# Attention stage: the turns of the outputs and of the row of maxima move from the maxima's banks to the scores' banks, and from VectorE to ScalarE and GpSimd

## The reference, cut to what matters

```python
q = (x @ wq.T).reshape(B, S, num_heads, D)      # B 2, S 2048, 16 heads, D 16; k and v alike
scores = jnp.einsum('bqhd,bkhd->bhqk', q, k) * scale
probs = jax.nn.softmax(scores, axis=-1)
out = jnp.einsum('bhqk,bkhd->bqhd', probs, v).reshape(B, S, H)
return out @ wo.T
```

## Time and profile before

| | us |
|---|---|
| median of three timed runs | 3472.24 |
| the profiled execution, its own time | 3464.76 |
| its span | 3464.1 |
| attention stage, first exponential to last write of `att` | 1270.9 to 2765.3 |

### The profile page before, as it was taken

The page is one execution under the profiler, slowest core; times in us unless marked ns, Lnnn a source line. Parts: engine busy times, 40 slices in busy tenths (PEclk is TensorE's granted clock), DMA queues, the critical chain, the costliest instruction groups (busy, mean ns, idle before and its releaser), DMA issues. The chain is left out here.

```text
span 3464.1 us, 45140 instructions
## 1 busy us (share of the span) xinstructions
PE 2931.5 (85%) x12880; PEld 1119.1 (32%) x12881; DVE 2463.2 (71%) x2802; ACT 1877.2 (54%) x3418; POOL 1049.5 (30%) x556
## 2 busy tenths in 40 slices
PE   5799899888776869999999999999999872999990
PEld 1234344433333412222222222222222252566650
DVE  0699999999995588888887888888888364111113
ACT  3656665666542427776776767676677710222220
POOL 2888878877861610000000000000000035100006
PEclk8999999999988969999999999999999975999995
DMA  1111111111112521111111111111111036111114
GB/s 41 43 49 55 38 49 55 49 40 49 49 37 74 184 64 38 34 30 31 29 38 38 38 38 29 38 37 38 29 27 29 14 113 230 48 45 45 45 36 144
DMA packets 123092, 185.24 MB, mean 53 GB/s; under 512 B 30224, under 2 KB 77968, under 8 KB 122896
## 3 DMA queue, kind: packets, MB, share of 16 engines
q1 hardware_dynamic: 109072, 142.95, 14.6%
q0 software_dynamic: 13824, 39.86, 3.6%
HBM read 138.01 MB, written 44.43 MB: 53 GB/s over the span
## 5 line engine op out<-in xcount | busy, mean ns | idle before, releaser
L1446 DVE TENSOR_REDUCE nmh<-ring 128x2 f32<-128x1024 f32 x1024 | 1191.0, 1218 | 242.3 <-PE ring L1336 241.1
L1323 ACT ACTIVATE prob<-s_ps 128x512 f32<-128x512 f32 x2048 | 1066.9, 601 | 479.2 <-PE s_ps L1360 478.2
L767 DVE TENSOR_TENSOR_SCAN h<-dA,state,bx 128x512 f32<-128x512 f32 x512 | 618.6, 1268 | 115.3 <-ACT dA L606 114.7
L391 POOL TENSOR_TENSOR bx<-u,bb 128x2048 f32<-128x2048 f32 x128 | 578.8, 4528 | 194.2 <-DVE h L767 194.0
L1360 PE MATMUL s_ps<-qs,ks 98*128 98x512 bf16 x2048 | 600.9, 390 | 21.4 <-issue 13.7
L1372 PE MATMUL acc<-prob,vst 128*32 128x512 f32 x4096 | 557.0, 616 | 0.7 <-ACT prob L1323 0.7
L606 ACT ACTIVATE dA<-dt,aneg 128x512 f32<-128x512 f32 x512 | 348.8, 691 | 271.1 <-DVE h L767 271.0
L673 PE MATMUL y_ps<-h,ident 128*128 128x512 f32 x1024 | 491.2, 625 | 1.1 <-DVE h L774 1.1
L1336 PE MATMUL ring<-k,q 64*128 64x512 bf16 x2048 | 375.5, 398 | 106.7 <-DVE att L1470 40.2
L1311 POOL COPY vst<-v_all 128x544 f32 (+1 forms) x16 | 10.2, 641 | 1358.4 <-PE acc L1372 1358.4
L1360 PEld LDWEIGHTS s_ps<-qs,ks 98*128 98x128 bf16 x2048 | 152.7, 98 | 508.7 <-ACT prob L1323 398.8
(11 more groups left out here) (218 smaller groups left out, 2466.0 us busy)
## 6 DMA issues: line engine op xcount, KB each, us to landing
bb<-b_rows SPq DMA_DIRECT2D x128, 256.0 KB, 3.1
q<-parts SPq DMA_DIRECT2D x256, 64.0 KB, 2.1
parts<-part POOLq DMA_DIRECT2D x48, 256.0 KB, 3.1
qs<-parts SPq DMA_DIRECT2D x192, 64.0 KB, 2.9
ks<-parts SPq DMA_DIRECT2D x192, 64.0 KB, 3.0
xt<-slots_in POOLq DMA_DIRECT2D x72, 128.0 KB, 2.3
slots_out<-yt SPq DMA_DIRECT2D x72, 128.0 KB, 1.7
k<-parts SPq DMA_DIRECT2D x256, 32.0 KB, 1.9
```

Source lines behind the costliest of these rows:

```text
L391: nc.gpsimd.tensor_tensor(bx[:, n % BR], u[:, b], bb[:, n % RB, None, :].to_broadcast([P, KI, CH]), ALU.mult).then_inc(s_bx, 1)
L767: nc.vector.tensor_tensor_scan(h[:, n % HR, d, :], dA[:, d % 2, :], bx[:, n % BR, d, :], state[:, b, n, d:d + 1], ALU.mult, ALU.add).then_ ...
L1323: nc.scalar.activation(prob[:, k % PR, j, :], s_ps[:, m % SR, :], ACT.Exp, scale=SC).then_inc(s_exp, 1)
L1446: nc.vector.tensor_reduce(nmh[:, slot, t, 2 * s:2 * s + 2], ring[:, s, :, :], AX.X, ALU.max, negate=True).then_inc(s_free[s], 1)
```

## The change

Both turns leave the ring and take their place in the sequence of score tiles. Each head now has `TILES` = 66 bank uses, 64 score tiles, tile `I_OUT` = 12 for the outputs' transposes and tile `I_ROW` = 53 for the transpose of the maxima, all on the three banks of `s_ps` in turn. ScalarE copies each turn out to SBUF (`oraw`, `rowf`) and counts it with the exponentials; it copies `acc` out, too. VectorE keeps the combination to `nm` and the reciprocal (from `oraw`). GpSimd makes the two bfloat16 parts of the row and the product into `att`; its copy of v's columns is made in the second head of the pair before. The diff, cut to its core (`taken` is the count of the exponential or copy that takes a tile; the special cases of the first and last head are left out):

```diff
+        T_OUT, T_ROW = 2, KT - LEAD
+        I_OUT = QC * (T_OUT + 1)
+        I_ROW = QC * (T_ROW + 1) + 1
+        TILES = QC * KT + 2
...
-            if has_prev:
-                steps[2].append((OUT, 0))
...
-                steps[KT - LEAD].append((ROWMAX, 0))
...
+        def tile_of(t, j):
+            return QC * t + j + (1 if t > T_OUT else 0) + (1 if t > T_ROW else 0)
...
+        def bank_free(head, tile):
+            back = tile - SR
...
+            return taken(head, back)
...  SyncE
-            def max_rows(par, hh, fills):
-                wait_apart(sp, s_free[0], fills, s_one)
+            def max_rows(head, par, hh):
+                wait_apart(sp, s_nmr, head + 1, s_one)
...  GpSimd
+            def rows_of_max(head, tiles, sent):
+                wait_apart(pool, s_exp, tiles, s_id)
+                if sent is not None:
+                    wait_apart(pool, sent[0], sent[1], s_id)
+                nc.gpsimd.tensor_copy(nmr[:, 0, :], rowf[:, :]).then_inc(s_hi, 1)
+                wait_apart(pool, s_hi, head + 1, s_id)
+                nc.gpsimd.tensor_tensor(nmr[:, 1, :], rowf[:, :], nmr[:, 0, :], ALU.subtract).then_inc(s_nmr, 1)
+
+            def outputs(n, hh):
+                wait_apart(pool, s_rec, 2 * n + hh + 1, s_id)
...
+                nc.gpsimd.tensor_tensor(dst, got[:, :, :, 0:HD], r[:, :, :, None].to_broadcast([P, TT, QC, HD]),
+                                        ALU.mult).then_inc(s_on, 1)
...
             def head(n, it, par, hh, has_prev, has_next, has_then):
-                if hh == 0:
-                    wait_apart(pool, s_pv, KK * (n - 1), s_id)
...
+                if hh == 1 and has_next:
+                    wait_apart(pool, s_pv, KK * n, s_id)
+                    columns(n + 1, 1 - par)
+                if has_prev:
+                    outputs(n if hh == 1 else n - 1, 1 - hh)
+                if has_next:
+                    rows_of_max(2 * n + hh + 1, taken(2 * n + hh, I_ROW), (s_mr[hh], 32 * (n + 1)))
...  ScalarE
+            def read_acc(n, hh):
+                wait(act, s_pv, KK * n + KT * (hh + 1))
+                nc.scalar.copy(osb[:, hh, :], acc[:, :]).then_inc(s_o, 1)
+
+            def take_output(head, tile, nth):
+                wait(act, s_S, taken(head, tile))
+                wait(act, s_on, nth)
+                nc.scalar.copy(oraw[:, :], s_ps[:, tile % SR, :]).then_inc(s_exp, 1)
+
+            def take_row(head, tile, nth):
+                wait(act, s_S, nth if tile < 0 else taken(head, tile))
+                wait(act, s_nmr, nth - 1)
+                nc.scalar.copy(rowf[:, :], s_ps[0:KT, tile % SR, 0:P]).then_inc(s_exp, 1)
...
+                    if t == 1 and has_prev:
+                        read_acc(n if hh == 1 else n - 1, 1 - hh)
...  the four exponentials of key tile t
+                    if t == T_OUT and has_prev:
+                        take_output(u, I_OUT, u - 1)
+                    if t == T_ROW and has_next:
+                        take_row(u, I_ROW, u + 2)
...  TensorE
+            def rows_of_max(head, tile, nth):
+                wait(pe, s_exp, bank_free(head, tile))
+                wait(pe, s_comb, nth)
+                nc.tensor.transpose(s_ps[0:KT, tile % SR, 0:P], nm[:, :], ident[:, :]).then_inc(s_S, 1)
+            def outputs(free, tile, n, hh):
+                wait(pe, s_exp, free)
                 wait(pe, s_o, 2 * n + hh + 1)
...  the four transposes, now into s_ps[:, tile % SR, ...], counted in s_S
                     scores(n, par, k, 2)
                     scores(n, par, k, 3)
+                    turn(t)
                     values_of_last(k)
...  VectorE
-                nc.vector.tensor_copy(nmr[:, 0, :], ring[0:KT, 0, 0, 0:P]).then_inc(s_nmr1, 1)
...  and the subtraction, the product into att and the copy of acc
+            def reciprocals(tiles, n, hh):
+                wait(dve, s_exp, tiles)
+                wait(dve, s_on, 2 * n + hh - 1)
...
+                    if t == T_OUT + 1 and has_prev:
+                        reciprocals(taken(u, I_OUT), n if hh == 1 else n - 1, 1 - hh)
```

More of the change, by code:

```diff
@@ L1181, in attention_stage, with plan @@
         LOADS4 = 16 * 2 * 2 * 4
-        MAXNEXT, MAXTHEN, ROWMAX, OUT = "maximum, next head", "maximum, head after", "rows of the maximum", "output"
-        def plan(has_prev, has_next, has_then):
+        MAXNEXT, MAXTHEN = "maximum, next head", "maximum, head after"
+        T_OUT, T_ROW = 2, KT - LEAD
+        I_OUT = QC * (T_OUT + 1)
+        I_ROW = QC * (T_ROW + 1) + 1
+        TILES = QC * KT + 2
+        assert TILES % SR == 0 and I_ROW - I_OUT > SR
+        def plan(has_next, has_then):
             steps = [[] for _ in range(KT)]
-            if has_prev:
-                steps[2].append((OUT, 0))
             if has_next:
@@ L1281, in head @@
                 if has_next:
[L1282 to L1291, removed]
+                    max_rows(2 * n + hh + 1, *next_head(n, par, hh)[1:])
             every_head(sp, prologue, head)
@@ L1315, in _ @@
+            every_head(pool, prologue, head)
+            outputs(NP - 1, 1)
         @block.scalar
         def _(act):
-            def head(n, it, par, hh, has_prev, has_next, has_then):
-                for k in range(hh * KT, (hh + 1) * KT):
+            def read_acc(n, hh):
[5 more added lines that the diff above has]
+                nc.scalar.copy(oraw[:, :], s_ps[:, tile % SR, :]).then_inc(s_exp, 1)
@@ L1368, in values @@
                     wait(pe, s_vst, n + 1)
-                wait(pe, s_exp, NU * n + QC * (k + 1))
+                wait(pe, s_exp, taken(2 * n + hh, tile_of(t, QC - 1)))
                 for j in range(QC):
@@ L1404, in use_ring, with turn @@
                             maxima(ct, hh, at, s)
[L1405 to L1409, removed]
+                def turn(t):
+                    if t == T_OUT and has_prev:
+                        outputs(bank_free(u, I_OUT), I_OUT, n if hh == 1 else n - 1, 1 - hh)
+                    if t == T_ROW and has_next:
+                        rows_of_max(u, I_ROW, u + 2)
                 def values_of_last(k):
@@ L1435, in epilogue @@
                 values(NP - 1, 1, KK - 1)
-                ct = Count(2 * NP - 1, last=True)
-                ct.next(1)
-                outputs(ct, NP - 1, 1)
+                outputs(TILES * 2 * NP - 1, 0, NP - 1, 1)
             every_head(pe, prologue, head, epilogue)
@@ L1447, in maxima, with rows_of_max @@
                                         negate=True).then_inc(s_free[s], 1)
-            def rows_of_max(ct, n, hh, sent):
+            def rows_of_max(ct, slot, turned):
                 for s in range(2):
                     wait(dve, s_free[s], ct.n[s])
[L1452 to L1455, removed]
-                nc.vector.tensor_copy(nmr[:, 0, :], ring[0:KT, 0, 0, 0:P]).then_inc(s_nmr1, 1)
[L1457 to L1464, removed]
+                wait(dve, s_exp, turned)
+                nc.vector.tensor_reduce(nm[:, :], nmh[:, slot, :, :], AX.X, ALU.min).then_inc(s_comb, 1)
+            def reciprocals(tiles, n, hh):
+                wait(dve, s_exp, tiles)
+                wait(dve, s_on, 2 * n + hh - 1)
+                got = oraw[:, :].rearrange("p (c j w) -> p c j w", c=TT, j=QC)
                 r = rec[:, hh, :].rearrange("p (c j) -> p c j", j=QC)
                 nc.vector.reciprocal(r, got[:, :, :, HD]).then_inc(s_rec, 1)
[L1467 to L1476, removed]
             def prologue():
```

106 lines of the change are left out of this document (58 added, 48 removed).

## The result

The changed kernel takes 3385.74 us (median of 4, 3382.51 to 3388.28), the kernel before 3472.59 on the same chip: the ratio is 0.9751, 95% interval 0.9737 to 0.9765. The profiled execution took 3382.51 us, its span is 3381.1, 83.0 less than before.

A forecast was written before the change was run, and what follows sets the result against it. TensorE's own row of work was taken to bound the undisturbed period; 40.2 + 28.8 + 9.6 + 14.2 = 92.8 us off 3464.76 gave 3372, with 7.5 us for the median 3379.5, say 3380 us; range 3360 to 3420.

The forecast's parts named there:

- Undisturbed period: Two key tiles of a head without a turn: 5.28 us, TensorE's own row of work, not touched by the change.
- Outputs' turn: Period with the outputs' transposes: 0.72 us extra in place of 2.06, gain 1.34 us in 30 heads, 40.2 us.
- Row's turn: Period with the transpose of the maxima: 0.30 us extra in place of 1.23, 0.93 us in 31 heads, 28.8 us.
- Copies on ScalarE: Copies of `acc`, outputs and row moved to ScalarE: 0.59 us each large, about 0.28 the row; ScalarE does not become the bound.
- The row's way: Row to `qs` through ScalarE, GpSimd and SyncE: lands at 7.0 us, 8.2 at the slowest, wanted at 11.1; no cost.
- The rival's place: Rival that the row comes late: TensorE waits for it at each head's start, kernel slower, up to 3507 us; chance 0.04.
- GpSimd: Product into `att` 0.57 us, the row's two operations 0.4 us each, all off the path; no cost.
- The wrap: Pair boundary, where a bank wraps too soon: 0.64 us saved 15 times, 9.6 us, since 66 tiles divide by 3.
- The clock: Nine drops of TensorE's clock behind outputs' stalls in the loop go: 9 x 1.58 = 14.2 us, the least certain term.
- its first rival: The clock keeps dropping: drops hang on the back edge and work around it, not the stall; 3394 us, chance 0.15.
- The ends: Start about 0.9 us less, end about 0.9 us more for a second ScalarE copy and hand-over: even.

The follow-up runs named there:

- the late row: The changed kernel with one added GpSimd operation of two inputs on 128 x 4096 elements ahead of the parts of the row: 3480.68 us, ratio 1.0026.
- the bank order: The kernel before with only the order of its three score banks changed, from score tile 10 of a pair on: 3468.98 us, ratio 0.9995.
- the new engines in the old place: The kernel before with ScalarE copying both turns and `acc` out and GpSimd finishing, both turns still in the ring: 3445.37 us, ratio 0.9928.
- the turns one place later: The changed kernel with each turn behind the values on TensorE instead of ahead of them: 3369.64 us, ratio 0.9703.

## Why the prediction was right

The forecast was 3380 us, the measurement 3385.74. Against the profiled execution the sum said 92.8 us; the span fell by 83.0. By the prediction's own steps:

- **Undisturbed period, 5.28 us, TensorE's own.** Right: eight periods of 5.28 us and what the two turns add make 42.24 + 0.75 + 0.37 = 43.36, the head measured.
- **Outputs' turn, 0.72 us for 2.06.** Measured 0.75. 30 x 1.31 = 39.3 us for 40.2. The transposes start 2.05 us into the period (2.06 reckoned), and the values follow them after 0.59 (0.55).
- **Row's turn, 0.30 us for 1.23.** Measured 0.37, 31 x 0.86 = 26.7 us for 28.8. The transposing instruction took 0.21 us to the next load (1391.63 to 1391.84), not the 0.13 taken over from the outputs.
- **Copies on ScalarE cost nothing.** Shown for the two large ones by doubling them: not even twice the work shows.
- **The row's way.** DMAs out at 3.93 us where 4.1 were reckoned, landing 1.7 us in the median again. The slack was reckoned at 4.1 us (11.1 - 7.0); the late row shows 4.6 in the mean. The rival's place was right: once the row is late enough, TensorE waits for it at the head's start.
- **GpSimd.** The product took 619 ns for the 570 taken, the parts of the row 279 and 417 for 400 each. The Trainium skill (GPSIMD Engine Reference, Elementwise — side-by-side cycle accounting) has GpSimd about two times slower with two inputs, measured there on 2048 elements. Here the product takes 619 ns for VectorE's 425 and the subtraction 417 for 278, a factor of 1.5; the cast, with one input, takes 279 ns on both. VectorE read PSUM and GpSimd reads SBUF, so this is not the same operation in all. It is off the path either way.
- **The wrap, 0.64 us.** 0.58 by the two traces of the bank order, 8.7 us for 9.6.
- **The clock, 14.2 us.** The weakest term, as said. All nine drops behind the outputs' stall went, as forecast, and with the stalls of 0.81 us they are gone, too. But the excess fell by 36.5 - 25.6 = 10.9 us only, as the heads with back edges have become no cheaper, rather some 2.5 us dearer in all. Two readings behind this term were wrong. The window 1590 to 1600 of the earlier trace rows is not of an unrolled head: the first back edge comes at 1638.87, so it lies in the loop's first pass. And only four of the five back edges are followed by a drop at once. What that window shows is a stall in the loop without a drop; the stalls of the unrolled heads, which the prediction held in favour of its first rival, are shorter (1.20 to 1.26 us). Nor do the drops belong to particular heads. There were 9 in the kernel before, 14 with another bank order, 3 with the loop written out, 1 with both.
- **The ends.** Taken as even. The first copy of `acc` comes 2.1 us earlier; but in the twelve traces it lies anywhere from 1316.5 to 1325, so this can't be told from chance. The last two heads together are 0.3 us longer.

The terms measured: 39.3 + 26.7 + 8.7 + 10.9 = 85.6 us; the trace's parts are 81.1 us over 29 head intervals, 2.1 at the start and -0.3 in the last two heads, 83.0 with the rounding. The terms count 30 and 31 turns, the intervals hold 29 of each, which is 3.0 us of the 4.5 between 85.6 and 81.1 (1.31 + 2 x 0.86). The median fell by 86.85 us, the span by 83.0; single runs differ by that much.

Open: why a stall of one and the same length drops the clock in some heads and not in others. The stall of 1.37 us drew a drop in 3 of 10 heads of the kernel before and in 11 of 14 with the other bank order. Which moment decides was not tried, nor why the stalls are longer in the loop. One of ten executions with the late row took 13271.89 us, one of the kernel before 7126.07; no trace was taken of these. The medians of their runs count them, the ratios do not.

## What to carry to other kernels

When a small job borrows a double buffer from a busy producer and consumer, ask which buffer's next user comes latest, before asking which engine is free: here the same engines in another buffer brought the whole gain, other engines in the old buffer less than a third, and more than half of that by way of the clock. Place such a job behind work that does not depend on the buffer, so that the buffer is free when its turn comes. And before a gain of a fraction of a microsecond in each round is given up as unmeasurable, count the rounds in which the clock fell: a stall kept elsewhere can eat it.

## What was not expected of the hardware

- Stalls of TensorE of 1.19 to 1.49 us were followed by a stretch at 1.2 GHz (some 1.5 us lost) in 1 to 14 of 30 cases, by the kernel: 5 of 74 up to 1.26 us, 22 of 46 from 1.31 us. Stalls of 0.81 us (the new engines in the old place) were followed by none in 30.
- GpSimd's two-input operation on 4096 elements took 7.01 us, 1.71 ns an element, while the one on 2048 took 4.53 us, 2.21 ns. Here both inputs were the same tile; that this is the reason was not tried.
- A back edge of the loop in the changed kernel cost 4.3 to 5.9 us in one head and the next (43.4 taken off each). TensorE waits 2.6 to 2.8 us of it for its next instruction, and all five are followed by a drop. With the turns one place later, two of five drew none and cost 2.7 us.
